# State-space block: frequency convolution over half the length with ten combined weights, C copied by ScalarE, half of its product on GpSimd

## What is computed

```python
xz = einsum('bld,ed->bel', hidden, in_proj_w)
out   = branch(xz, forward weights)              # below
out_b = branch(xz[:, :, ::-1], backward weights)
x, z = split(xz)
xf = fftn(x, axes=(-2, -1))                      # over channels and length
xc = concatenate([xf.real, xf.imag], axis=1)     # 512 channels x 256
xc = conv(xc, fft_conv_w, 5 taps, padding 2)     # 512 -> 512 channels
xc = silu(xc + fft_conv_b)
x_out = ifftn(complex(*split(xc)))
out_f = normalize(abs(x_out * max(silu(z))))
y = out + out_b[:, :, ::-1] + out_f
result = einsum('bdl,od->blo', y, out_proj_w)

# branch: x, dt, B, C from projections; for 16 states n, 256 channels d:
h[t] = exp(delta[t] * A) * h[t-1] + delta[t] * B[t] * x[t]
y[t] = sum over n of h[t] * C[t] + D * x[t];  y * silu(z)
```

## Time and profile before

| what | value |
|---|---|
| median of 3 runs | 2163.7 us (2162.97 to 2166.92) |
| span of the profiled execution | 2167.6 us |
| PE busy, share of the span | 2020.1 us, 93% |
| DVE busy | 1686.2 us, 78% |
| ACT busy | 1374.7 us, 63% |
| POOL busy | 1112.7 us, 51% |
| DMA, bytes moved | 144.94 MB |

### The profile page before, as it was taken

How to read it: one execution, slowest core, us unless ns; L and a number is a source line. 1 busy time by engine, 2 the same in 40 slices (tenths; PEclk the granted TensorE clock), 3 DMA queues, 4 the chain that set the end, 5 groups by cost and what they waited for, 6 DMA issues and landing times. The chain is left out here.

```text
span 2167.6 us, 40610 instructions
## 1 busy us (share of the span) xinstructions
PE 2020.1 (93%) x14620; PEld 1506.8 (70%) x14620; DVE 1686.2 (78%) x2918; ACT 1374.7 (63%) x2687; POOL 1112.7 (51%) x1509
## 2 busy tenths in 40 slices
PE   6999999986999995999999988699999999999878
PEld 4677777754887773677777755577877877877745
DVE  5777777765888875777777765499999999999974
ACT  1677777763777773677777653467586685685633
POOL 3555555623767764555555512345736647556423
PEclk8899999997999997999999997899999999999989
DMA  4655566530000003555555515000000000000000
GB/s 133 148 149 147 146 148 149 145 106 1 2 2 2 2 2 78 151 149 146 149 145 150 150 31 200 1 1 1 1 1 1 1 1 0 1 0 1 1 15 20
DMA packets 147750, 144.94 MB, mean 67 GB/s; under 512 B 14048, under 2 KB 106976, under 8 KB 146912
## 3 DMA queue, kind: packets, MB, share of 16 engines
q1 hardware_dynamic: 127968, 132.91, 22.4%
q10 hardware_dynamic: 19584, 9.44, 2.4%
HBM read 94.07 MB, written 38.80 MB: 61 GB/s over the span
## 5 line engine op out<-in xcount | busy, mean ns | idle before, releaser
L606 DVE TENSOR_REDUCE sb_f_mx<-ps_f_s 128x2 f32<-128x512 f32 x768 | 506.4, 686 | 216.5 <-PE ps_f_s L354 215.6
L530 ACT ACTIVATE sb_f_pt<-ps_f_t 128x1024 f32<-128x1024 f32 x384 | 382.1, 1023 | 114.9 <-issue 56.2
L1954 POOL TENSOR_TENSOR sb_mb_h<-sb_mb_h 128x512 f32<-128x512 f32 x128 | 165.0, 1310 | 303.4 <-DVE sb_mb_h L1837 302.3
L354 PE MATMUL ps_f_s<-sb_f_stack 96*128 96x256 bf16 x1536 | 286.5, 279 | 22.1 <-DMA sb_f_stack<-f_scr 14.1
L1832 DVE TENSOR_TENSOR_SCAN sb_mb_h<-sb_mb_da,sb_mb_h 128x1024 f32<-128x1024 f32 x128 | 304.4, 2418 | 2.7 <-ACT sb_mb_da L1692 2.7
L1503 PE MATMUL ps_mb_f<-sb_mb_fc,sb_mb_cw 128*128 128x256 f32 x1280 | 286.8, 381 | 6.7 <-ACT sb_mb_fc L1705 6.6
L1503 PEld LDWEIGHTS ps_mb_f<-sb_mb_fc,sb_mb_cw 128*128 128x128 f32 x1280 | 239.7, 190 | 41.4 <-ACT sb_mb_fc L1705 8.9
L371 PE MATMUL ps_f_t<-sb_f_stack 128*128 128x256 bf16 x1536 | 232.9, 274 | 6.3 <-ACT sb_f_pt L530 3.3
L1692 ACT ACTIVATE sb_mb_da<-sb_mb_dl,sb_mb_an 128x255 f32<-128x255 f32 x512 | 211.0, 496 | 31.3 <-DVE sb_mb_h L1832 30.7
L354 PEld LDWEIGHTS ps_f_s<-sb_f_stack 96*128 96x128 bf16 x1536 | 140.7, 99 | 109.7 <-issue 41.3
L427 PE MATMUL ps_f_a<-sb_f_pt,sb_f_v 128*32 128x256 f32 x3072 | 188.8, 387 | 1.6 <-ACT sb_f_v L579 1.6
(11 more groups left out here) (252 smaller groups left out, 4132.7 us busy)
## 6 DMA issues: line engine op xcount, KB each, us to landing
f_scr<-sb_f_parts SPq DMA_DIRECT2D x96, 384.0 KB, 2.7
sb_f_stack<-f_scr SPq DMA_DIRECT2D x192, 192.0 KB, 3.0
sb_f_stack<-f_scr SPq DMA_DIRECT2D x192, 128.0 KB, 3.1
sb_f_stack<-f_scr SPq DMA_DIRECT2D x192, 64.0 KB, 3.3
sb_f_stack<-sb_f_mrow ACTq DMA_DIRECT2D x96, 96.0 KB
sb_mb_cw<-in_cw SPq DMA_DIRECT2D x1, 5120.0 KB, 19.4
sb_prep_wn<-in_wn SPq DMA_DIRECT2D x6, 512.0 KB, 7.7
sb_m_w<-in_w SPq DMA_DIRECT2D x6, 256.0 KB, 3.1
```

The costliest lines, as they stand in the source:

```text
L354: last = nc.tensor.matmul(s_bank[j % 2][:, h, :], stack[0:ROWS, a.n % STACKS, 0, g * GROUP + pair * 2 + h, half * P:(half + 1) * P], stack ...
L530: nc.scalar.activation(pt[:, e.two, g, half, :, :], t_bank[i % 2][:, :, :], ACT.Exp).then_inc(s["pt_sb"], 1)
L606: nc.vector.tensor_reduce(mx[:, a.two, half, head:head + 2], s_bank[j % 2][:, :, :], AX.X, ALU.max)\
L1954: nc.gpsimd.tensor_tensor(hb[:, c, 0:2, :], hb[:, c, 0:2, :], hb[:, c, 2:4, :], ALU.add).then_inc(s["half_sb"], 1)
```

## The change

Four things are changed together.

1. **Half length.** The convolution runs over half of the frequencies. ACT writes the two transforms of half the length (`even`, `odd`) into a new tile `fold`, POOL's new `neighbours` adds or subtracts shifted and reversed columns of it (eight instructions of about 2 x 129 elements in each partition, in slots 1 to 3, ahead of that slot's products), and PE does 10 x 2 x 4 = 80 products with 128 to 131 columns in place of 80 with 256, in seven pieces over slots 1 to 4. ACT copies one part of the result (`diff`), DVE's new `unfold` (two instructions of 508 elements, in unit 5 between scans and product) forms the full length by sum and difference, and ACT's `gate_frequency` applies Silu in slot 6.
2. **Ten combined weights.** They are sums and differences of mirrored weights: POOL forms them in the attention phase in 38 instructions of 512 elements in each partition, from 10 MB that SP loads at its start, and SP stores them in ten DMAs of 512 KB to a scratch in DRAM, from which `cw` is loaded as before.
3. **C copied by ScalarE.** ACT's new `expand` copies `c_bank` (1024 elements) into the SBUF tile `csb` at the start of each slot, after both products of the unit before.
4. **Half of its product on GpSimd.** DVE multiplies only chunk 1 by C, from `csb`; POOL's `products` multiplies chunk 0, and adds the four states to two in each chunk; PE's `total` adds the two left over, with four products in place of two.

```diff
+        def joined(step):
+            return max(0, (step - 4) * (SUMS + JOINS) // (len(steps) - 4))
+        @block.sync
+        def _(sp):
+            for i in range(2 * DC):
+                sp.dma_start(wa[:, p, c, :, :], d["cwa"][:, p, c, :, :]).then_inc(raw[i], 16)
+                sp.dma_start(wb[:, p, c, :, :], d["cwb"][:, p, c, :, :]).then_inc(raw[i], 16)
...
+            for a in range(1, len(FOLDS)):
+                sp.wait_ge(s["wfold_sb"], 2 * a)
+                sp.dma_start(d["cw"][:, a, :, :], wf[:, a, :, :]).then_inc(s["w_stored"], 16)
+            sp.wait_ge(s["w_stored"], 16 * len(FOLDS))
...
+                for i in range(joined(step), joined(step + 1)):
+                    combine(i)
...
                     for j in range(PIECES[piece], PIECES[piece + 1]):
+                        a, n = divmod(j, DC * XC_CH)
+                        ic, oc = divmod(n, XC_CH)
+                        at, cols, to = FOLDS[a]
+                        if a >= 2 and n == 0:
+                            pe.wait_ge(s["fold_sb"], m.b * (len(FOLDS) - 2) + a - 1)
+                        last = nc.tensor.matmul(f_both[:, oc // 2, oc % 2 * N + to:oc % 2 * N + to + cols],
+                                                cw[:, a, ic, oc * P:(oc + 1) * P], fold[:, ic, at:at + cols],
...
+            def expand(m, un):
+                n = m.b * UNITS + un + 1
+                act.wait_ge(s["c_ps"], n)
+                since(act, "hc_sb", n - 1)
+                since(act, "hp_sb", n - 1)
+                nc.scalar.activation(csb[:, :, :], c_bank[:, :, :], ACT.Copy).then_inc(s["csb_sb"], 1)
...
+            def gate_frequency(m):
+                act.wait_ge(s["split_sb"], m.b + 1)
+                for oc in range(XC_CH):
+                    last = nc.scalar.activation(fs[:, oc, :], fs[:, oc, :], ACT.Silu, bias=cb[:, oc:oc + 1])
...
                 for slot in range(UNITS):
+                    if m:
+                        expand(m, slot)
+                    if m and slot == 6:
+                        gate_frequency(m)
...
-                dve.wait_ge(s["c_ps"], n)
-                for c in range(DC):
-                    dve.wait_ge(s["scan_sb"], DC * (n - 1) + c + 1)
-                    nc.vector.tensor_tensor(hb[:, c, :, :], hb[:, c, :, :], c_bank[:, :, :], ALU.mult).then_inc(s["hc_sb"], 1)
+                if un == 5:
+                    unfold(m)
+                dve.wait_ge(s["csb_sb"], n)
+                dve.wait_ge(s["scan_sb"], DC * n)
+                nc.vector.tensor_tensor(hb[:, 1, :, :], hb[:, 1, :, :], csb[:, :, :], ALU.mult).then_inc(s["hc_sb"], 1)
+            def unfold(m):
+                dve.wait_ge(s["f_sb"], FREQ * m.b + 4)
+                both = f_split[:, :, :, HALF_N - 1:0:-1]
+                nc.vector.tensor_tensor(fs4[:, :, :, 1:HALF_N], both, diff, ALU.add)
+                nc.vector.tensor_tensor(fs4[:, :, :, N - 1:HALF_N:-1], both, diff, ALU.subtract).then_inc(s["split_sb"], 1)
...
-            def halve(m, un):
...
+            def products(m, un):
+                n = m.b * UNITS + un + 1
+                hb = h[:, (n - 1) % HBUFS, :, :, :]
+                pool.wait_ge(s["csb_sb"], n)
+                pool.wait_ge(s["scan_sb"], DC * (n - 1) + 1)
+                nc.gpsimd.tensor_tensor(hb[:, 0, :, :], hb[:, 0, :, :], csb[:, :, :], ALU.mult).then_inc(s["hp_sb"], 1)
+                pool.wait_ge(s["hp_sb"], n)
+                nc.gpsimd.tensor_tensor(hb[:, 0, 0:2, :], hb[:, 0, 0:2, :], hb[:, 0, 2:4, :], ALU.add).then_inc(s["half_sb"], 1)
+                pool.wait_ge(s["hc_sb"], n)
+                nc.gpsimd.tensor_tensor(hb[:, 1, 0:2, :], hb[:, 1, 0:2, :], hb[:, 1, 2:4, :], ALU.add).then_inc(s["half_sb"], 1)
...
+                    if m and un in (1, 2, 3):
+                        for a in range(3 * un - 1, min(3 * un + 2, len(FOLDS))):
+                            neighbours(m, a)
                     if m:
-                        halve(m, un)
+                        products(m, un)
```

More of the change, by code:

```diff
@@ L1401, in mamba_phase @@
         y_bank = k.psum("mb_y", [P, DC, N], ctx)
-        f_bank = [k.psum(f"mb_f{i}", [P, 512], ctx) for i in range(2)]
+        f_both = k.psum("mb_f", [P, 2, 512], ctx)
+        f_bank = [f_both[:, i, :] for i in range(2)]
+        f_split = f_both[:, :, :].rearrange("p a (b n) -> p a b n", b=2)
         w_bank = k.psum("mb_w", [P, 2, N], ctx)
@@ L1516, in frequency @@
                         last.then_inc(s["f_ps"], 1)
-                elif slot == 7 and half == 1:
-                    pe.wait_ge(s["f_sb"], seen + 5)
-                    for dc in range(DC):
-                        for c in range(XC_CH):
-                            ri, kc = divmod(c, 2)
-                            last = nc.tensor.matmul(f_bank[(1 + dc) % 2][:, :],
-                                                    uk[:, kc, ri * CH_I + dc * P:ri * CH_I + (dc + 1) * P], gi[:, c, :],
-                                                    start=c == 0, stop=c == XC_CH - 1)
-                    last.then_inc(s["f_ps"], 1)
+                elif slot == 7:
+                    dc = half
+                    if dc == 0:
+                        pe.wait_ge(s["f_sb"], seen + 6)
+                    for c in range(XC_CH):
+                        ri, kc = divmod(c, 2)
+                        last = nc.tensor.matmul(f_bank[dc], uk[:, kc, ri * CH_I + dc * P:ri * CH_I + (dc + 1) * P], gi[:, c, :],
+                                                start=c == 0, stop=c == XC_CH - 1)
+                    if dc == 1:
+                        last.then_inc(s["f_ps"], 1)
             def spread(m, un, which):
                 r, g = divmod(un, SU)
-                bank, name, read = ((b_bank, "b_ps", "dbu_sb"), (c_bank, "c_ps", "hc_sb"))[which]
+                bank, name, read, each = ((b_bank, "b_ps", "dbu_sb", DC), (c_bank, "c_ps", "csb_sb", 1))[which]
                 if un == 0 and m.b == 0:
@@ L1535, in spread @@
                     pe.wait_ge(s["bc_sb"], 2 * m.b + 2)
-                since(pe, read, DC * (m.b * UNITS + un))
+                since(pe, read, each * (m.b * UNITS + un))
                 for i in range(SG):
@@ L1579, in combine @@
             def combine():
-                for part in range(2):
-                    cols = w.gm[:, :, 0:2, :] if part == 0 else w.gm[:, :, 2:3, :]
-                    for c in range(DC):
-                        last = nc.tensor.matmul(f_bank[part][:, 0:(2 - part) * CH_I], winr[:, c, :],
-                                                cols[:, c, :, :].rearrange("p t n -> p (t n)"), start=c == 0, stop=c == DC - 1)
+                for c in range(DC):
+                    last = nc.tensor.matmul(f_bank[0][:, 0:CH_I], winr[:, c, :], w.gm[:, c, :], start=c == 0, stop=c == DC - 1)
                 last.then_inc(s["gw_ps"], 1)
```

262 lines of the change are left out of this document (165 added, 97 removed).

## The result

The changed kernel takes 2272.3 us (median of 4 runs, 2267.6 to 2277.8) against 2163.3 (2162.6 to 2166.9) for the kernel before: a ratio of 1.0498 with a 95% interval of 1.0485 to 1.0511. The forecast was 2265.

The account below looks back on a forecast made before the run. DVE sets the pace of the state-space phase, PE nearly as full; 84.0 us per sequence becomes 96.5, +100 over 8 sequences, and +2 in attention gives 2265 us from 2163.7, range 2195 to 2325.

Parts of the forecast that it names:

- What POOL and DVE do to each other: State-space phase: a POOL instruction and a DVE instruction with two SBUF inputs exclude each other for their whole length.
- The sum, 96.5 per sequence: State-space phase, one sequence: 84.0 + 10.4 + 4.2 − 2.1 = 96.5 us.
- ACT: Copy of C, +8.2 us of ACT work a sequence; lateness tight at slot 7's: 0 in sum, up to +3.
- third rival: ACT-PE chain late by 3 us at slot 7's expand, PE clock loss 3; signs: that releaser, clock under 0.95; +150, 13%.
- POOL: Each unit: DVE's product waits behind POOL's half product, 2.2 us; a unit 10.2 against 8.89, +10.4 per sequence.
- Reliefs: Per sequence: −1.0 where DVE has other work, −1.1 where neighbours push POOL's product under products with B.
- second count: All DVE and POOL work per sequence that must exclude each other: 89.1 us at least, 97.3 with full records.
- neighbours: Eight POOL instructions in slots 1 to 3 take turns with scans: +4.2 us per sequence, bounds 0 and 5.9.
- unfold: DVE in unit 5, before the wait for POOL's product: 0, or +1.2 us if that cover is gone.
- PE: Shorter convolution leaves PE some 74 us of 96.5 per sequence; off the path, so the gain is worth nothing.
- Attention phase: Weight combining, 38 POOL instructions, 48 us: costs 0 to 5 us, taken as +2.
- faster rival: POOL's product does not hold DVE up: 76.2 us per sequence, −62, 2104 us; DVE waits under 0.45 per unit; 7%.

Follow-up runs that it names:

- e7: Kernel before with only ScalarE's copy of C, GpSimd's half product and four products in total; convolution at full length: 2227.4 us (1.0288).
- e3: Changed kernel, VectorE's product reads C from PSUM; PE's spreading of C waits for it, ScalarE's copy no longer: 2219.6 us (1.0257).
- e4: Changed kernel with GpSimd's product left out; ScalarE's copy of C no longer waits for it: 2181.9 us (1.008).
- e9: As e8, and ScalarE copies the convolution's result at the head of slot 5 and applies Silu at its end: 2238.2 us (1.0321).
- e8: Changed kernel with the output projection ahead of slot 6's inverse transform, and the ScalarE copy it needs ahead of the copy of C: 2249.2 us (1.0374).
- e2: Changed kernel without ScalarE's copy of C and GpSimd's product; VectorE multiplies both chunks from PSUM: 2214.8 us (1.023).
- e5: Changed kernel with each of the eight neighbours instructions per sequence cut to one column of each range: 2256.8 us (1.0424).
- e6: Changed kernel with each of the convolution's 80 products on TensorE made twice: 2281.9 us (1.0533).
- e12: As e11, with spreading of C behind each slot's frequency work, squares after decay factors, energies after unit 0: 2158.0 us (0.9955).
- e11: As e2, with the output projection ahead of the inverse transform and the early Silu: 2195.4 us (1.0129).

## Why the prediction was right, and where it was off

**What POOL and DVE do to each other.** Right. The records of the changed kernel and of e7 show it (4.18 beside 3.12, 4.19 beside 3.13), and the record of e3, 1.22, shows that it goes with the operand. End to end it is 90.4 us for GpSimd's product (e4) and 62 for that half of the change alone (e7); e3's 52.7 has a moved wait in it. The plain product with both inputs in SBUF waits like `steps`: the Trainium skill (SBUF — State Buffer, Who interferes with whom) gave it alone, and now the rows agree, 3.12 us against 1.22 from PSUM.

**The sum, 96.5 per sequence, came out as 97.7, but by terms that make up for one another.** That the total is so near is partly luck. e9 has the exclusion without the late chain: 93.2, so +9.2 where the steps added 12.5. The chain is the other 4.5 (97.7 − 93.2).

**The missing term: the chain through ACT and PE.** Under *ACT* I put "0 in the sum, up to +3", and I looked for it at `expand` of slot 7. It was late at slot 6, and the price fell on `project_out`. I had listed what is queued behind `expand` ("Silu, `front`, `decay`") and weighed only `decay`. Whoever waits for the Silu is PE, and whoever stands behind PE's transform is `project_out`. Taken away in e8 and e9 together it is worth 34 us of 2272. So the third rival's mechanism was there as well, in part, beside the likeliest, and one of its two signs came: a clock under 0.95 (0.93 over the launch). The clock's share is seen at the transform, 78.5 us for L1577 against 56.3 for the same work before (its L1513), 2.8 per sequence, and it falls where DVE waits. In e2 it took 57.6 us and `add_output` still waited 37.4 us, so the larger part is the order.

**Too large: *POOL* and *Reliefs*.** By the forecast GpSimd's product costs 17.6 less 2.1 per sequence; e4 says 11.3, with a wait of ScalarE in it. The wait of 2.2 us under the second scan was put into each of eight units. The durations of the product tell that it is not so (ns, least, median and most):

```profile
L2048 POOL TENSOR_TENSOR sb_mb_h<-sb_mb_h,sb_mb_csb x64: 2338/2355/4332, 1414.6 to 2183.0; 128x1024 f32<-128x1024 f32 x64
```

The median is the bare price, 2355 ns: in more than half of the units GpSimd, late with its other work, has its turn at once. What VectorE has to wait then depends on what it asks for. Three units of one repetition of the changed kernel:

```profile
1625.39 2.35 POOL L2048 TENSOR_TENSOR sb_mb_h<-sb_mb_h,sb_mb_csb 128x1024 f32<-128x1024 f32 x1
...
1636.95 2.35 POOL L2048 TENSOR_TENSOR sb_mb_h<-sb_mb_h,sb_mb_csb 128x1024 f32<-128x1024 f32 x1
1637.48 1.83 DVE L1974 SCALAR_TENSOR_TENSOR sb_mb_nm<-sb_mb_mv,sb_mb_rs 128x2 f32<-128x2 f32 x1
...
1669.44 2.34 POOL L2048 TENSOR_TENSOR sb_mb_h<-sb_mb_h,sb_mb_csb 128x1024 f32<-128x1024 f32 x1
1669.62 3.25 DVE L1921 TENSOR_TENSOR sb_mb_h<-sb_mb_h,sb_mb_csb 128x1024 f32<-128x1024 f32 x1
```

In the first VectorE is at instructions with at most one input in SBUF (from 1626.28 the products with B) and waits for nothing; in the second `combine` waits 1.8 us, in the third the product with C waits 2.2. In slot 6 (1682.38 above) VectorE stood idle. So of the eight units some cost nothing and some the forecast's price. What is pushed back is paid under the scans as well: in e9 two of them take up to 7.46 us, with two additions of 3.13 and 3.25 beside them.

```profile
1581.64 2.35 POOL L2052 TENSOR_TENSOR sb_mb_h<-sb_mb_h,sb_mb_csb 128x1024 f32<-128x1024 f32 x1
1581.90 7.46 DVE L1919 TENSOR_TENSOR_SCAN sb_mb_h<-sb_mb_da,sb_mb_h 128x1024 f32<-128x1024 f32 x2
1584.08 3.13 POOL L2054 TENSOR_TENSOR sb_mb_h<-sb_mb_h 128x512 f32<-128x512 f32 x1
1587.17 3.25 POOL L2056 TENSOR_TENSOR sb_mb_h<-sb_mb_h 128x512 f32<-128x512 f32 x1
```

The forecast's second count, which adds what must exclude each other, gave 89.1 to 97.3 and held e9's 93.2 in its middle. Here it was the better method, because it does not ask where in the queue a wait falls.

***neighbours*.** 4.2 per sequence in the sum, 1.9 by e5; e5 keeps eight short instructions (579 ns on average), so the true figure is more, by how much no run says. ***unfold*.** Its 0 hung on POOL's product as cover. In slot 5 that product started only at 1669.44, as `unfold` ended (1669.70), so it was no cover, and the other end of the bound, 1.2 us, is the likelier price. No run has it alone.

**PE.** 74 us of work became 79.5 busy, at a clock of 0.90, and off the path as said (e6: 9.6 us for 154 more). e12 has the 74.2 at 0.96.

**Attention phase.** +2 predicted, +2.4 measured.

**The faster rival** asked that DVE wait less than 0.45 us per unit for POOL; the rows show 2.14 in a unit, and e4 the price. Two slips in the working change nothing: its sum comes to 2103, not 2104, and an addition of 256 elements is 0.71 us by the earlier trace rows, not 0.73.

The stretch between the attention phase and the state-space phase, whose code the change does not touch, is 2.9 us shorter in the trace of the changed kernel (545.2 against 548.0). In the traces of the experiments it lasts 541.8 to 547.7 us, so this is scatter between executions, and so may be a part of the attention phase's +2.4 (+1.2 to +4.1 in those traces).

## What to carry to other kernels

Price a moved operation twice: by what the two engines exclude of each other in a whole repetition, which is a sum and does not depend on where the queue stands, and then by following, for each wait that is added, every instruction behind it on its engine to the one who needs it, and who stands behind that one in turn. When a measured total agrees with the forecast, look at the idle time all the same: here 4.5 us of an unforeseen wait per sequence stood in for 3.3 that had been overpriced, and following the wait led to a kernel faster than both. An edit whose gain lies off the path (here 133 us of TensorE's time) pays only when all that it adds is hidden: with the split product the half-length convolution came with a loss of 5%, and with C left in PSUM and three queues put in order with a gain of 0.45%.

## What the runs showed that I had not expected

Even the smallest VectorE instruction with two SBUF inputs waits out a GpSimd instruction. In the changed kernel the product of two columns in `combine` (L1974) took 1446 ns on average, one of them 1.83 us beside a GpSimd product that ended with it (at 1637.48 above), and 160 ns in e11, where GpSimd had little to do; `join` took 2352 against 824 (the changed kernel's line, then that of e11):

```profile
L1982 DVE SCALAR_TENSOR_TENSOR sb_mb_ys<-sb_mb_ys,sb_mb_vv 128x512 f32<-128x512 f32 x8 | 18.8, 2352 | 1.2 <-ACT sb_mb_vv L1841 1.2
...
L1985 DVE SCALAR_TENSOR_TENSOR sb_mb_ys<-sb_mb_ys,sb_mb_vv 128x512 f32<-128x512 f32 x8 | 6.6, 824 | 1.2 <-ACT sb_mb_vv L1843 1.2
```

A removed wait gives back less than its length when another engine used it to catch up: 50 us of wait gone in e8, 23 us of time won. And TensorE, idle for 5.25 and 3.15 us in slots 5 and 6, ran one half of a transform in 6.74 us at a granted clock of 0.53, and the equal half 7.5 us later in 3.60 at 1.00.
